# The last stages of a graph layer with an LSTM: two half-scans joined in one scan in token order, and the residual's 2h added during the sweeps

## The reference

```python
_, hs = jax.lax.scan(step, (h0, c0), ...)        # LSTM over the 6250 tokens
logits = einsum('bth,lh->btl', h, W_lin) + b_lin # two classes
g = argmax(logits)                               # 0 or 1 for each token
w = g * h
inc = cumsum(w, axis=1)
prefix = inc - w
suffix = inc[:, -1:, :] - inc
out = x1 + 2.0 * h + prefix * fw_att + suffix * bw_att
```

## Time and profile before

| | |
|---|---|
| median of 3 runs | 2064.66 us (2064.16 to 2067.29) |
| the profiled execution's own time | 2065.32 us |
| its span | 2063.5 us |
| busy: PE, DVE, ACT, POOL | 1866.5, 1539.1, 1127.8, 229.7 us |
| last step of the loop ends | 1951.86 us into the span |
| first work on TensorE after the loop | 1959.76 us |
| scans | 1988.27 to 2014.52 us |
| output stage | 2014.80 us to the end |

### The profile page before, as it was taken

How to read it: one execution, slowest core, us unless ns; L and a number is a source line. 1 busy time by engine, 2 the same in 40 slices (tenths; PEclk the granted TensorE clock), 3 DMA queues, 4 the chain that set the end, 5 groups by cost and what they waited for, 6 DMA issues and landing times.

```text
span 2063.5 us, 42573 instructions
## 1 busy us (share of the span) xinstructions
PE 1866.5 (90%) x13524; PEld 1595.8 (77%) x13524; DVE 1539.1 (75%) x4189; ACT 1127.8 (55%) x3147; POOL 229.7 (11%) x283
## 2 busy tenths in 40 slices
PE   5688998999999999999999899997779999999745
PEld 4467886888888888888888788886569999999733
DVE  7977888777777777777739867777876666666697
ACT  4475444444444444444434456666876666666527
POOL 3353001110011001101112200000000000000070
PEclk8799998999999999999999999999999999999975
DMA  5222321100111010101044122223443334333303
GB/s 135 86 85 76 96 94 47 35 30 31 31 32 32 28 33 28 36 25 36 28 141 120 56 80 112 107 119 129 169 150 110 131 130 129 111 128 127 110 0 124
DMA packets 95699, 170.39 MB, mean 83 GB/s; under 512 B 8213, under 2 KB 67369, under 8 KB 95296
## 3 DMA queue, kind: packets, MB, share of 16 engines
q1 hardware_dynamic: 66029, 84.75, 12.5%
q10 hardware_dynamic: 27248, 77.11, 11.5%
q0 software_dynamic: 2320, 7.26, 1.1%
HBM read 110.53 MB, written 58.56 MB: 82 GB/s over the span
## 4 chain that ended last, share of the span: by engine, by line
PE 63%; DVE 18%; ACT 8%; issue 7%; POOL 2%; DMA 1%; ACTq 0%; DVEq 0%; SPq 0%; POOLq 0%
PE psum L683 27%; PE psum L837 15%; PE psum L678 7%; PE psum L794 5%; ACT scr L1144 2%; DVE scr L1535 2%; DVE scr L1738 2%; DVE bufB L1664 2%; ACT scr L1112 1%; DVE bufA L1868 1%; PE psum L627 1%; PE psum L653 1%; DVE bufA L1860 1%; DVE bufB L1755 1%; DVE scr L1338 1%
## 5 line engine op out<-in xcount | busy, mean ns | idle before, releaser
L1560 DVE TENSOR_TENSOR wx<-rs_buf 128x392 bf16<-128x392 bf16 (+1 forms) x1568 | 497.0, 389 | 163.8 <-PE psum L678 160.0
L683 PE MATMUL psum<-halves,counts 128*128 128x512 f32 x2401 | 599.8, 399 | 0.7 <-ACT counts L1050 0.7
L683 PEld LDWEIGHTS psum<-halves,counts 128*128 128x128 f32 x2401 | 437.5, 189 | 85.4 <-issue 0.9
L1050 ACT ACTIVATE counts<-psum 128x392 fp32r<-128x392 f32 x784 | 327.4, 505 | 273.5 <-PE psum L678 272.1
L837 PE MATMUL psum<-bufB,wx 128*128 128x125 f32 x3392 | 408.9, 279 | 17.0 <-DVE bufB L1755 12.0
L837 PEld LDWEIGHTS psum<-bufB,wx 128*128 128x128 f32 x3392 | 390.6, 191 | 35.3 <-issue 20.9
L678 PEld LDWEIGHTS psum<-wx 128*128 128x128 bf16 x3136 | 157.9, 98 | 39.6 <-issue 20.8
L678 PE MATMUL psum<-wx 128*128 128x98 bf16 x3136 | 184.1, 210 | 4.0 <-DVE wx L1560 2.9
L794 PE MATMUL psum<-bufA,wx 128*128 (+1 forms) x800 | 180.1, 376 | 3.1 <-POOL rs_buf L544 3.1
L794 PEld LDWEIGHTS psum<-bufA,wx 128*128 128x128 f32 x800 | 146.6, 188 | 20.1 <-issue 3.3
L1738 DVE TENSOR_TENSOR scr<-scr 128x125 f32<-128x125 f32 x280 | 81.2, 290 | 103.8 <-ACT scr L1144 96.9
(11 more groups left out here) (260 smaller groups left out, 2488.8 us busy)
## 6 DMA issues: line engine op xcount, KB each, us to landing
bufA<-gates_of_x ACTq DMA_DIRECT2D x136, 500.0 KB, 3.4
gates_of_x<-bufB SPq DMA_DIRECT2D x24, 1000.0 KB, 3.9
x_times_eps_plus_sums<-scr SPq DMA_DIRECT2D x50, 128.0 KB, 1.7
sums_by_feature<-scr SPq DMA_DIRECT2D x50, 128.0 KB, 1.9
scr<-x_times_eps_plus_sums SPq DMA_DIRECT2D x49, 128.0 KB, 2.0
wx<-in_x_dram SPq DMA_DIRECT2D x25, 250.0 KB
x_plus_mix<-wx SPq DMA_DIRECT2D x25, 250.0 KB, 4.5
bufB<-sums_by_feature SPq DMA_DIRECT2D x21, 250.0 KB, 3.0
```

Of the source, the lines that this page charges most:

```text
L683: return mm(psum[:, 3 + v, :], cnt[v][:, hi, :], xhl[:, hi, :, :].rearrange("p s d -> p (s d)"), start=(hi == 0), stop=(hi == NT - 1))
L1050: fn(cnt[v][:, :, c * u:c * (u + 1)], psum[:, CB[u % 4], 0:PER * KEYS].rearrange("p (c h) -> p h c", h=NT), ACT.Copy).then_inc(S["c_sb"], 1)
L1560: last = tt(to, tab2[:, 0:k_, :].unsqueeze(1).broadcast_to([P, PER // 2, k_, 2]), keysT[v][:, part_, g0:g0 + PER // 2, :].unsqueeze(2).bro ...
```

## The change

The work after the loop is divided in another way:

- **Residual.** During the loop's 50 steps GpSimd makes 2h of the step just done (`twice_h`) and adds it to the residual's columns of that step: `x1h = x1T + 2h`, written to bufA (`add_twice`, two instructions a step). ScalarE no longer doubles `hs`. `pre_in` moves from bufA to `wx`. GpSimd gets a While loop of its own, and VectorE waits for GpSimd's last addition before it writes `flag`.
- **Logits.** `lin_rep` has a place of its own and is made in the first sweep (`difference`). A block is now 250 tokens in token order (five chunks), so TensorE reads `hs` with a step of 252 floats (`h_of`).
- **Gate.** VectorE writes only the mask (`masked`), one instruction of 250 a block; GpSimd multiplies h by it for both halves at once, 500 elements a partition, and writes w in token order into `cum`, now in bufC.
- **Scan.** ScalarE makes `in_fw = fw * w` one token back and `in_bw = -bw * w`, the latter with its sum as a second output (`scaled`, four instructions a block). VectorE runs s = in_fw + s + in_bw over each block of 250, starting from the last column of the block before (`sums`, two a block). So s = fw * prefix - bw * inc, and the sum over all blocks gives `tbw`. VectorE does the scan of block i - 3 after the mask of block i.
- **Output.** A result is (s + tbw) + x1h, two VectorE instructions a block. Four results and four PSUM banks instead of two, six row buffers instead of four.

```diff
-        cum = bufA[:, 0:2 * (N + 1)].rearrange("p (c n) -> p c n", c=2)
+        cum = bufC[:, 0:2 * (N + 1)].rearrange("p (c n) -> p c n", c=2)
+        x1h = bufA[:, 0:2 * N].rearrange("p (c n) -> p c n", c=2)
+        twice_h = scr[:, 2816:2816 + HC].rearrange("p (c j) -> p c j", c=2)
+        in_fw, in_bw = ([scr[:, 512 * v:512 * v + 2 * BN].rearrange("p (c n) -> p c n", c=2) for v in pair] for pair in ((0, 1), (2, 3)))
...
+        def h_of(b, c):
+
+            return hs[:, :, c, b * JB:(b + 1) * JB].rearrange("p t j -> p j t")
...                                                          (GpSimd)
-            pool.wait_ge(S["twice_act"], NB)
-            for i in range(NB):
-                cells = x1T[:, :, i * BN:(i + 1) * BN].rearrange("p c (j t) -> p c j t", t=LS)
-                for c in range(2):
-                    pool.tensor_tensor(cells[:, c, :, :], cells[:, c, :, :], hs[:, 0:LS, c, ...], ALU.add)
+            def add_twice(before, row):
+
+                pool.wait_ge(S["hh_v"], before + (2 * row + 4))
+                if row > CUT:
+                    pool.wait_ge(S["xh_q"], before + 2 * (row - LS - CUT))
+                pool.tensor_tensor(twice_h, hs[:, row % LS, :, :], hs[:, row % LS, :, :], ALU.add).then_inc(S["xh_q"], 1)
+                pool.wait_ge(S["xh_q"], before + (2 * (row - LS - CUT) + 1))
+                pool.tensor_tensor(steps_of(x1h, row % LS), steps_of(x1T, row % LS), twice_h, ALU.add).then_inc(S["xh_q"], 1)
...
+            with pool.While(lambda: pool.snap(go) > pool.snap(k_r_)):
+                for row in range(CUT, CUT + LS):
+                    add_twice(before, row)
+                pool.wait_ge(S["flag_v"], kv + 1)
...
+            pool.memset(cum[:, :, 0:1], 0.0).then_inc(S["w_q"], 1)
             for i in range(NB):
+                pool.wait_ge(S["mask_v"], i + 1)
+                pool.tensor_tensor(cum[:, :, i * BN + 1:(i + 1) * BN + 1].rearrange("p c (j t) -> p c j t", t=LS),
+                                   hs[:, :, :, i * JB:(i + 1) * JB].rearrange("p t c j -> p c j t"),
+                                   mask[i % MASKS].unsqueeze(1).broadcast_to([P, 2, BN]).rearrange("p c (j t) -> p c j t", t=LS),
+                                   ALU.mult).then_inc(S["w_q"], 1)
...                                                          (TensorE)
-            mm(psum[0:1, 5, 0:1], ones[:, 0:1], ones[:, 0:1], start=True, stop=True).then_inc(S["pe_swept"], 1)
-                    last = mm(psum[:, LGB[i % 4], 0:BN], lin_rep[:, k, :], hs[:, ds(2 * i, 2), k, :],
+                    last = mm(psum[:, LGB[i % 4], 0:BN].rearrange("p (j t) -> p j t", t=LS), lin_rep[:, k, :], h_of(i, k),
...                                                          (ScalarE)
-                fn(hs[:, 2 * i:2 * i + 2, :, :], hs[:, 2 * i:2 * i + 2, :, :], ACT.Copy, scale=2.0).then_inc(S["twice_act"], 1)
-                    last = fn(suf[par][:, c, 0:out_cells(i)], cum[...], ACT.Identity, bias=tbw[:, c:c + 1], scale=nbw[:, c:c + 1])
+            def scaled(i):
+
+                act.wait_ge(S["w_q"], i + 2)
+                if i >= 2:
+                    act.wait_ge(S["cum_v"], 2 * (i - 2) + 3)
+                for c in range(2):
+                    fn(in_fw[i % 2][:, c, :], cum[:, c, i * BN:(i + 1) * BN], ACT.Copy, scale=fwc[:, c:c + 1])
+                for c in range(2):
+                    last = fn(in_bw[i % 2][:, c, :], cum[:, c, i * BN + 1:(i + 1) * BN + 1], ACT.Copy, scale=nbw[:, c:c + 1],
+                              accum_out=w_part[:, c, i:i + 1])
...                                                          (VectorE)
+                dve.wait_ge(S["xh_q"], kv * (2 * LS) + 2 * LS)
                 dve.wait_ge(S["cnt_mm"], kv + 1)
                 ts(flag[0:1, :], psum[0:1, 6, 400:401], P - 0.5, float(CH), ALU.is_lt, ALU.mult).then_inc(S["flag_v"], 1)
...
-                    last = stt(cum[:, c, 1:N + 1].rearrange("p (j t) -> p t j", t=LS)[:, ds(2 * i, 2), :], psum[...], b_d[:, 0:1],
-                               hs[:, ds(2 * i, 2), c, :], ALU.is_gt, ALU.mult)
-                dve.tensor_tensor_scan(cum[:, c, 1:N + 1], psum[:, 4, 0:1].broadcast_to([P, N]), cum[:, c, 1:N + 1], 0.0,
-                                       ALU.mult, ALU.add).then_inc(S["cum_v"], 1)
+                ts(mask[i % MASKS], psum[:, LGB[i % 4], 0:BN], b_d[:, 0:1], None, ALU.is_gt).then_inc(S["mask_v"], 1)
+                    dve.tensor_tensor_scan(cum[:, c, i * BN:(i + 1) * BN], in_fw[i % 2][:, c, :], in_bw[i % 2][:, c, :],
+                                           cum[:, c, i * BN - 1:i * BN] if i else 0.0, ALU.add, ALU.add).then_inc(S["cum_v"], 1)
+            LAG = 3
+            for i in range(NB + LAG):
+                if i < NB:
+                    masked(i)
+                if i >= LAG:
+                    sums(i - LAG)
...
-                    stt(res[par][:, c, 0:w], cum[:, c, ds(i * ON, w)], fwc[:, c:c + 1], x1T[:, c, ds(i * ON, w)], ALU.mult, ALU.add)
-                tt(res[par][:, :, 0:w], res[par][:, :, 0:w], suf[par][:, :, 0:w], ALU.add).then_inc(S["t_v"], 1)
+                    stt(res[u][:, c, 0:w], cum[:, c, ds(i * ON, w)], tbw[:, c:c + 1], x1h[:, c, ds(i * ON, w)],
+                        ALU.add, ALU.add).then_inc(S["t_v"], 1)
```

More of the change, by code:

```diff
@@ L50 @@
 RING = 8
-LGB = (6, 7, 2, 3)
+LGB = (7, 6, 2, 3)
+OUTB = (0, 1, 4, 5)
 CB = (0, 1, 2, 7)
@@ L175, in build @@
         blc = cols[:, 12:14]
-        nbw, tbw = sb("nbw", 2), sb("tbw", 2)
+        nbw, tbw, w_sum = sb("nbw", 2), sb("tbw", 2), sb("w_sum", 2)
         lin_c = sb("lin_c", 4)
-        lin_rep = wih[:, 0:2 * P].rearrange("p (a m) -> p a m", a=2)
+        lin_rep = rs_buf[:, 2 * HC:2 * HC + 2 * P].rearrange("p (a m) -> p a m", a=2)
         lin_d, b_d = sb("lin_d", 2), sb("b_d", 1)
@@ L441, in _ @@
                     rows_to(i, even, out_cells(i) // 2)
-            for v in range(4):
-                sp.wait_ge(S[f"out_st{v}"], 16 * ((NO + 3 - v) // 4 + (1 if v == (NO - 1) % 4 else 0)))
+            for v in range(OUTS):
+                sp.wait_ge(S[f"out_st{v}"], 16 * ((NO + OUTS - 1 - v) // OUTS + (1 if v == (NO - 1) % OUTS else 0)))
         @block.gpsimd
@@ L731, in _ @@
             pe.wait_ge(S["ld_w12"], 32)
-            pe.wait_ge(S["eps1_v"], 3)
+            pe.wait_ge(S["vec_v"], 2)
             def tail(i, par, inner=False):
@@ L934, in _, with rows @@
             for i in range(NB):
-                logits(i, i < 4)
-            def rows(i, par, first):
-                pe.wait_ge(S["t_v"], 3 * i + 3)
+                logits(i)
+            def rows(i, u, first):
+                pe.wait_ge(S["t_v"], 2 * i + 4)
                 if not first:
-                    pe.wait_ge(S["out_act"], i - 1)
+                    pe.wait_ge(S["out_act"], i - 3)
                 w = out_cells(i)
@@ L1771, in _, with difference @@
             c_left = [c[:, :, 0:CH] for c in c_wide]
+            def difference(stage):
+                if stage == 0:
+                    tt(lin_d[:, :], lin_c[:, 2:4], lin_c[:, 0:2], ALU.subtract).then_inc(S["vec_v"], 1)
+                    tt(b_d[:, :], blc[:, 0:1], blc[:, 1:2], ALU.subtract).then_inc(S["vec_v"], 1)
+                else:
+                    dve.wait_ge(S["vec_v"], 4)
+                    dve.tensor_copy(lin_rep, lin_d[:, :].unsqueeze(2).broadcast_to([P, 2, P])).then_inc(S["vec_v"], 1)
             def later_step(base, before, t):
@@ L1778, in later_step @@
                 fill(1 - u, loaded[1 - u] if t < LS - 1 else kept[0])
+                if isinstance(base, int) and base == 0 and t in (CUT, CUT + 1):
+                    difference(t - CUT)
                 sweep_step(base + t if isinstance(base, int) else dve.snap(base + t), t, u)
@@ new lines, in _, with results @@
+            LAG = 3
[4 more added lines that the diff above has]
+                    sums(i - LAG)
+            dve.tensor_reduce(w_sum[:, :], w_part, AX, ALU.add).then_inc(S["t_v"], 1)
+            dve.wait_ge(S["t_v"], 1)
+            ts(tbw[:, :], w_sum[:, :], -1.0, None, ALU.mult).then_inc(S["t_v"], 1)
+            dve.wait_ge(S["t_v"], 2)
+            dve.wait_ge(S["cum_v"], 2 * NB + 1)
+            def results(i, u, first):
@@ L1891, in _ @@
+            for i in range(RES):
+                results(i, i, True)
+            with dve.Fori(1, (NO - 1) // RES) as r:
+                for u in range(RES):
+                    results(RES * r + u, u, False)
             results(NO - 1, 0, False)
```

123 lines of the change are left out of this document (52 added, 71 removed).

## The result

The change made the kernel slower: 2075.49 us (2074.22 to 2076.42) against 2067.26 for the kernel before on the same chip, ratio 1.0044, 95% interval 1.003 to 1.0057. The forecast was 2058, worked out from a median of 2064.66; the other 2.6 us of the distance are the kernel before itself, which took 2067.26 here.

What follows compares the result with a forecast made beforehand. The sweeps were taken as bound by a nearly full TensorE in a closed ring of waits, with a four-link chain after the loop. Terms -21.5 + 11.0 + 4 + 0.8 = -5.7 us led to 2058 us, range 2040 to 2076.

Steps and rivals of the forecast that it cites:

- Output stage, -21.5 us: After tbw: 27.1 us instead of 48.6, at 0.93 us a block set by TensorE's transposes; gain 21.5 us.
- Gate and scan, +11.0 us: Combined stage after the loop: 2.44 us a block, ending at 2025.9 instead of 2014.9; loss 11.0 us.
- Exclusion: Combined stage: a two-SBUF-input scan and GpSimd's multiply cannot run together; 2.44 us a block instead of 1.9.
- mask and ScalarE fit beside it: Combined stage: VectorE's mask (0.47 us) and ScalarE's instructions (1.98 us) add nothing to the 2.44 us block.
- leaving the loop: After the sweeps: GpSimd's own loop exit costs nothing if under the 7.6 us to its first multiply.
- Sweeps, +4 us: Loop steps: GpSimd's second addition delays VectorE's forget 0; 8 us worked out, half taken, bounds 0 and 18.
- on the ring: Sweep step: closed chain of waits where delay is paid every step; 0.16 of forget 0's 0.30 us delay stays.
- the cover: Sweep step: slack between add 0's end and its tanh, hiding some 0.14 us of forget 0's delay.
- the sweeps pay: Loop steps: the strided second addition holds forget 0 fully, 0.16 to 0.36 us a step; 16 us, 2070 us; chance 0.24.
- Loop's end, +0.8: Before flag: VectorE waits for GpSimd's last addition, which the comparison's two-input instructions hold off; 0.8 us.
- TensorE's strided reading: Combined stage: logits reading hs 1008 bytes apart might take 3.3 us a block, 22 us longer, 2080 us; chance 0.08.

Runs made afterwards that it cites:

- short mask: The changed kernel with the mask written for only 16 of a block's 250 tokens, most of the gating left out: 2072.47 us, ratio 1.0038 to the kernel before.

## Why the prediction was wrong, step by step

- **Output stage, -21.5 us: right in kind, measured -25.0.** The first block and the end behind the last copy were as forecast (2.7 and 2.6 us); the 24 blocks between took 18.3 us instead of 22.0. Two prices were too high. At the halved clock, which held up to 2055.2, the four transposes of a block followed each other in 0.85 us, not 0.93, and VectorE's pair took 0.82, not 0.88, so half of the difference is there without any change of clock. The rest is that the halved clock was taken for granted over the whole stage: it rose to 1.00 after six copies, and the block went to 0.79. The stores followed at 340 GB/s with a DMA share of 0.92, against 0.40 at 151 in the earlier trace rows: the share scaled.
- **Gate and scan, +11.0 us: right mechanism, half the size, measured +22.5.** Exclusion was right, shown by putting one scan input in PSUM. The multiply (1.50 us) was priced well, the scans nearly so (0.725 us once nothing holds them, forecast 0.655). The failed sentence is "mask and ScalarE fit beside it": the mask is in the ring, with 0.37 us from its start to the scan's, which is nearly the 0.40 by which the block exceeds 2.44 us; the short mask took 0.19 of them away, and the block fell by 0.17. From the first multiply on this is 71.8 us instead of 63.5. The other 3.2 us are GpSimd's first multiply, 5.85 us after TensorE's start instead of 2.64: leaving the loop was called covered up to 7.6 us, and took 10.8. With masks made ahead it is worth 1.8 us at the end.
- **Sweeps, +4 us: the other step that failed, measured +10.5, of which the additions are 9.3 and the stretch of low clock, which no forecast had, 1.8.** The working gave 8 us (0.16 a step) and the text then took half, on the thought that the port might be given back once the inputs are read. No row spoke for that. Forget 0 came 0.32 us late, 0.20 of it on the ring. The addition ended 1.69 us after leave 1 (forecast 1.65), so its price was right; forget 0 ended 0.13 behind it (forecast 0.15); the cover was 0.12 instead of 0.14. This is the rival "the sweeps pay", and its threshold of 0.2 us a step was met, but its 16 us, from 0.32 a step, were too many, and its 2070 has the gate and scan at half their size.
- **Loop's end, +0.8: measured +0.9.**
- **TensorE's strided reading**, a rival with 0.08, was there and hidden: the estimate was 2.2 us a block at half clock, and the rows show 1.8 at either level. The Trainium skill, Advanced Engine Details and Errata, section SBUF Cachelines, gives no size for the penalty; this case's rows give 633 against 372 ns for 250 columns read 1008 bytes apart. At a granted clock of 0.50 the difference is small: with TensorE full, VectorE's first blocks follow each other 1.82 us apart strided (masks at 1973.35 and 1975.17) and 1.66 dense (1962.75 and 1964.41).
- **Exclusion itself.** The Trainium skill, SBUF — State Buffer, section Who interferes with whom, has the condition that the runs bore out for the scan: two SBUF inputs of VectorE exclude GpSimd, one does not (1250 to 725 ns), and a one-element broadcast counts as one of the two. One input is not always harmless: the earlier trace rows show another kind of instruction held with one. For plain products of 125 elements the runs show the first half only: 0.61 us beside GpSimd's addition and 0.29 without it; none was run with an input in PSUM.

The sum of the measured terms, 10.5 + 0.9 + 22.5 - 25.0, is the 8.9 us of the spans; forecast was -5.7. The gate and scan is the larger miss (11.5 us), enough by itself to turn the sign of the sum; the sweeps add 6.5, and the output stage hid 3.5 of both. That the time still lies inside 2040 to 2076 is luck: the upper end stood there for 16 us of sweeps. The runs that undo single parts agree in time: without the second addition 12.6 us less (11.4 by the ratios; 14.0 between the spans, which are 9.3 of sweeps, 0.9 of the loop's end, 1.8 of clock and some 2 of GpSimd's late start), and 24.7 less (23.3) without the scans' second SBUF input.

## What to carry to other kernels

When GpSimd gets work beside VectorE, list VectorE's instructions with two SBUF inputs in its path, and see where GpSimd's end falls against their start: here a piece that ended before them was free, and one that ended 0.5 us after their start cost 0.2 us in each of 50 steps. Moving one of the scans' inputs to PSUM gave all of their loss back (23 to 25 us), for one line of code. Work of VectorE on which GpSimd waits, here the mask, belongs into the sum of the block with its length, wherever it stands in the queue. And an estimate that comes out of the rows is not to be halved on a thought that no row supports.

## What the runs showed of the hardware that was not expected

- In the kernel before with its 1.0 in SBUF, a gapless GpSimd stream of 848 ns additions held one VectorE scan back for 23.5 us, to the stream's end; in short alternating work (scan, multiply, scan) the two took turns.
- GpSimd left its While loop 1.5 us after the flag with one instruction a step, and 10.8 to 11.1 us after it with two, whatever their size, and 9 instead of 4 instruction-loading packets lay in that stretch.
- ScalarE's sum output has an instruction of its own (186 ns), most of it beside its neighbours: of two activations without it the second adds 0.41 us (0.90 for the pair), and with it the next one begins 0.49 us after the first (1990.37 to 1990.86), so it costs some 0.08 us.
